# A GNN, MoE and routed-MLP megakernel on one core: the first expert's rows loaded early and finished by one-hot products; the last stage's row forms in halves, its relus' numbers loaded ahead, and one projection moved

## What is computed

```python
# step 2: experts; every token goes to one of E = 8, in the order of the tokens, at most C = 640 of each
idx = jnp.argmax(softmax(x @ gate_w + gate_b), axis=-1)
one_hot = jax.nn.one_hot(idx, E)
pos = (jnp.cumsum(one_hot, axis=0) * one_hot).sum(-1).astype(jnp.int32) - 1
buf = zeros((E, C, D)).at[idx, where(pos < C, pos, C)].set(x, mode='drop')
hmid = relu(einsum('ecd,edf->ecf', buf, w1) + b1)
ybuf = einsum('ecf,efd->ecd', hmid, w2) + b2          # then gathered back, times the probability
# step 3: x = x + adj @ (layernorm(x) * W)
# step 4: 64 segments of 64 rows, each with one of 16 experts in both layers
h = relu(flat @ Wi.T + bi)
for l in range(2):
    h = relu((h @ Ws[l] + bs[l]) + (h @ Wr[l, route].T + br[l, route]) + h)
out = h @ Wo.T + bo
```

## Time and profile before

| | |
|---|---|
| three runs | 974.94, 978.54, 980.27 us; median 978.54 |
| profiled execution | 976.39 us, its span 974.7 us |
| PE, DVE, ACT, POOL busy | 97%, 59%, 36%, 20% of the span |
| granted PE clock, mean | 0.988 of full speed |

### The profile page before, as it was taken

The page is one execution under the profiler, slowest core; times in us unless marked ns, Lnnn a source line. Parts: engine busy times, 40 slices in busy tenths (PEclk is TensorE's granted clock), DMA queues, the critical chain, the costliest instruction groups (busy, mean ns, idle before and its releaser), DMA issues.

```text
span 974.7 us, 15621 instructions
## 1 busy us (share of the span) xinstructions
PE 949.3 (97%) x4730; PEld 546.1 (56%) x4738; DVE 572.9 (59%) x1603; ACT 351.0 (36%) x845; POOL 195.3 (20%) x216
## 2 busy tenths in 40 slices
PE   8999999999999999999999899989999999999997
PEld 4555555555555544444443488834666666666665
DVE  5434234234224366777667388557886776877834
ACT  3554564564561022221111254414123333333242
POOL 3210010010010121122222246543120111102101
PEclk9999999999999999999999799979999999999999
DMA  9995784484303698988878257637998989989761
GB/s 354 422 412 198 320 345 174 172 346 195 151 1 136 261 374 318 348 313 318 317 293 357 75 167 244 209 90 287 380 375 323 371 319 341 353 317 360 231 185 52
DMA packets 64625, 263.26 MB, mean 270 GB/s; under 512 B 8852, under 2 KB 24920, under 8 KB 52246
## 3 DMA queue, kind: packets, MB, share of 16 engines
q1 hardware_dynamic: 61398, 257.69, 70.2%
q0 software_dynamic: 2864, 4.39, 1.3%
q10 hardware_dynamic: 272, 0.13, 0.0%
HBM read 244.37 MB, written 20.01 MB: 271 GB/s over the span
## 4 chain that ended last, share of the span: by engine, by line
PE 74%; DVE 9%; issue 5%; DMA 4%; DVEq 3%; ACT 3%; POOL 1%; ACTq 0%; another core or an unknown queue 0%; SPq 0%; POOLq 0%
PE PA L1893 22%; PE PA L2126 17%; PE PA L1873 11%; PE O L2064 3%; PE O L2230 3%; PE O L1942 3%; DMA disp_d<-work 2%; ACT U L800 2%; PE O L1914 2%; PE SM L2230 1%; PE SR L2230 1%; PE T L2241 1%; PE PA L1860 1%; PE O L1904 1%; PE O L2207 1%
## 5 line engine op out<-in xcount | busy, mean ns | idle before, releaser
L1893 PE MATMUL PA<-ring,S 128*128 128x512 f32 x512 | 229.0, 596 | 2.8 <-DMA ring<-in_adj_cols 2.3
L1873 PE MATMUL PA<-ring,U 128*128 128x512 f32 x512 | 223.3, 593 | 0.1
L1873 PEld LDWEIGHTS PA<-ring,U 128*128 128x128 f32 x512 | 96.0, 190 | 113.9 <-issue 113.8
L1893 PEld LDWEIGHTS PA<-ring,S 128*128 128x128 f32 x512 | 96.6, 191 | 105.3 <-issue 101.5
L2127 PE MATMUL PA<-ring 128*64 128x256 f32 x560 | 129.4, 380 | 0.0
L710 ACT ACTIVATE work<-ring 128x2048 int8<-128x2048 f32 x64 | 122.3, 1910 | 8.9 <-issue 4.7
L2126 PE MATMUL PA<-ring,S 128*64 128x256 f32 x448 | 105.4, 381 | 0.6 <-DVE ring L1704 0.6
L2126 PE MATMUL PA<-ring 128*64 128x256 f32 x336 | 80.6, 379 | 0.0
L2126 PEld LDWEIGHTS PA<-ring,S 128*64 128x64 f32 x448 | 60.0, 137 | 33.3 <-issue 3.9
L2127 PEld LDWEIGHTS PA<-ring 128*64 128x64 f32 x560 | 75.9, 137 | 0.0
L766 ACT ACTIVATE work<-work 128x128 f32<-128x128 f32 x112 | 33.2, 297 | 107.1 <-DVE work L1369 107.1
(11 more groups left out here) (305 smaller groups left out, 1448.1 us busy)
## 6 DMA issues: line engine op xcount, KB each, us to landing
ring<-in_adj_cols SPq DMA_DIRECT2D x52, 2048.0 KB, 9.7
ring<-in_adjT_cols SPq DMA_DIRECT2D x32, 2048.0 KB, 8.9
ring<-w_d SPq DMA_DIRECT2D x128, 256.0 KB, 3.7
ring<-in_adj_cols SPq DMA_DIRECT2D x8, 1024.0 KB, 14.2
ring<-in_Wr SPq DMA_DIRECT2D x4, 2048.0 KB, 8.9
w_d<-ring SPq DMA_DIRECT2D x8, 1024.0 KB
work<-in_w SPq DMA_DIRECT2D x16, 256.0 KB
disp_d<-U SPq DMA_DIRECT2D x4, 650.0 KB, 19.1
```

The source lines that it names most:

```text
L1873: mm = nc.tensor.matmul(out_T[:, :], X[:, t * D:(t + 1) * D], ring[slot][t // HT][:, (t % HT) * BW:(t % HT + 1) * BW], start=n == 0, stop= ...
L1893: mm = nc.tensor.matmul(PA[k % 2][:, :], S[:, t * D:(t + 1) * D], ring[slot][t // HT][:, (t % HT) * BW:(t % HT + 1) * BW], start=t == 0, s ...
```

## The change

1. **First expert.** When the scatters of the first seven blocks have landed, SP loads expert 0's slots (the rows of seven blocks; the last block's are still zero) into what was `gate_rows`. PE turns these five tiles with ordinary products into T[0], T[1] right after `tail_c`, ahead of the one `keep_warm` and `tail_d` (`early_turn`). POOL writes 0..639 into `e_slots` (iota) once the second layer's products are done, and the last block's four scatters now also wait for the early load. After `idx`, DVE compares the slots of each of the last block's four tiles with 0..639 (four comparisons, 128x640, `e_late`). PE, after `tail_d` and two `keep_warm` products, adds the last block's rows into T[0], T[1] by products with these one-hot rows (`late_rows`: for each tile 512 and 128 columns). The twelve `keep_warm` products and `turn_rows(0, 0)` go. SP waits for `late_rows` before it loads expert 1's weights. Expert 1's rows are turned in the middle of expert 0's second layer, not ahead of it. DVE adds two slices of shared weights ahead of the first expert, then one after each of experts 0 to 5.
2. **Row forms** are made in two halves: the first 16 tiles after `moments_y`, the second 16 after block 1's first quarter forms.
3. **Relus' numbers**: `relu_group` reads all four numbers ahead of its wait.
4. **Last block**: the `keep_warm` between the halves goes; `out_proj(7)` moves from ahead of layer 1 to behind `turn_routed(8, 1)`, into O[0]; block 8's layers both use SR and SM; `out_rows3(7)` moves behind layer 1's relus on DVE; the addition of the variance's epsilon moves from POOL to DVE.

```diff
             sp (after the loads of Wr)
+            sp.wait_ge(s_sc, 16 * BT * (NB - 1))
+            sp.dma_start(tiles(early_rows, CT, ROW), disp_t[:, 0:CT, :]).then_inc(s_early, 16)
             sp.wait_ge(s_sc, 16 * NT)
...
             load_rows(1, 1)
+            sp.wait_ge(s_xTp, 1)
             load_weights(1, 1)
             pool (step2)
+                    if nth == 2 * NB - 1:
+                        pool.wait_ge(s_agg2, NB)
+                        nc.gpsimd.iota(e_slots, pattern=[[1, CAP]], base=0, ...).then_inc(s_slots, 1)
                 if k == NB:
                     pool.wait_ge(s_rows, 1)
+                    pool.wait_ge(s_early, 16)
             dve (route)
+                if k == NB:
+                    nc.vector.scalar_tensor_tensor(slot_all, over, NOWHERE, slot_f, ALU.mult, ALU.add)
+                    dve.wait_ge(s_slots, 1)
+                    for t in range(BT):
+                        nc.vector.tensor_scalar(e_late[t], e_slots, slot_all[:, t:t + 1], None, ALU.is_equal).then_inc(s_late, 1)
...
-            for i in range(4):
+            for i in range(2):
                 add_self(i)
...
-                if e + 4 < NS:
-                    add_self(e + 4)
+                if e + 2 < NS:
+                    add_self(e + 2)
             pe (last2)
                 tail_c(k)
+                early_turn()
                 keep_warm(1, S[:, 0:BW], PA[0])
                 tail_d(k)
+                keep_warm(2, S[:, 0:BW], PA[0])
+                late_rows()
+            def early_turn():
+                pe.wait_ge(s_early, 16)
+                for q in range(CT):
+                    nc.tensor.matmul(slots_of(q), early_rows[:, q * ROW:q * ROW + D], ident[:, :], start=q % BT == 0, stop=False, ...)
+            def late_rows():
+                pe.wait_ge(s_rows, 1)
+                for t in range(BT):
+                    pe.wait_ge(s_late, t + 1)
+                    row = rows[:, t * ROW:t * ROW + D]
+                    nc.tensor.matmul(T[0][:, :], row, e_late[t][:, 0:BW], ...)
+                    last = nc.tensor.matmul(T[1][:, 0:CAP - BW], row, e_late[t][:, BW:CAP], ...)
+                last.then_inc(s_xTp, 1)
-            keep_warm(12, S[:, 0:BW], PA[0])
-            turn_rows(0, 0)
             pe (last3)
                 turn_hn3_half(0)
-                keep_warm(1, S[:, 0:BW], PA[1])
                 turn_hn3_half(1)
                 h0_half(0)
                 h0_half(1)
-                out_proj(NB - 1)
                 layer(k, 0)
                 turn_routed(k, 0)
                 turn_routed(k, 1)
+                out_proj(NB - 1)
                 layer(k, 1)
             dve (last stage)
-            row_forms()
+            row_forms(0)
             sum_forms(1, 0)
             cross_forms(1, 0)
             second_forms(1, 0)
             third_forms(1, 0)
+            row_forms(1)
             act (relu_group)
+                slots = [n % SB for n in range(g * SH, (g + 1) * SH)]
+                chosen = [act.value_load(...) for s in slots]
+                act.wait_ge(s_rt, (k - 1) * NG + g + 1)
+                for s, e in zip(slots, chosen):
```

More of the change, by code:

```diff
@@ L171, in build @@
         assert at + BW <= WORK
+        early_rows = gate_rows[:, 0:CT * ROW]
+        slot_all = limit
         BY_ROWS = range(1, NB)
@@ L189, in build @@
         e_hm = U[:, CAP:(1 + FK) * CAP]
+        e_late = [U[:, CAP * (1 + t):CAP * (2 + t)] for t in range(BT)]
+        e_slots = U[:, CAP * 5:CAP * 6]
         e_y = [R[:, CAP * i:CAP * (i + 1)] for i in range(2)]
@@ L622, in _ @@
             load_rows(1, 1)
+            sp.wait_ge(s_xTp, 1)
+            alone(sp)
             load_weights(1, 1)
@@ L844, in relu_group @@
                 dst = (h_b, h_a)[l]
[L845 to L850, removed]
+                slots = [n % SB for n in range(g * SH, (g + 1) * SH)]
+                chosen = [act.value_load(route_sb[0:1, ds((k - 1) * SB + s, 1)], min_val=0, max_val=E2 - 1) for s in slots]
+                act.wait_ge(s_rt, (k - 1) * NG + g + 1)
+                alone(act)
+                for s, e in zip(slots, chosen):
                     for m in range(KH):
@@ L1040, in _ @@
                 some = slice(h * H2, (h + 1) * H2)
-                inv_sqrt(H2, mv8[:, some, 1], s_mv4, NB + h, s_rstd4, first_power + NB + h, ve[:, some], rstd[:, some])
+                pool.wait_ge(s_mv4, NB + h)
+                alone(pool)
+                nc.gpsimd.tensor_tensor(rstd[:, some], ve[:, some], neg_half[:, 0:1].to_broadcast([P, H2]), ALU.pow).then_inc(s_rstd4, 1)
             store_rows(NB - 1)
@@ L1654, in last_hn3 @@
                     dve.drain()
-                    stats(lambda t: x3[:, t * D:(t + 1) * D], (h + 1) * H2, h * H2).then_inc(s_mv4, 1)
+                    stats(lambda t: x3[:, t * D:(t + 1) * D], (h + 1) * H2, h * H2)
+                    dve.drain()
+                    some = slice(h * H2, (h + 1) * H2)
+                    nc.vector.tensor_scalar(ve[:, some], mv8[:, some, 1], LN_EPS, None, ALU.add).then_inc(s_mv4, 1)
                 for h in range(2):
@@ L1670, in last_hn3, with row_forms @@
                         relu_rows(NB, g)
-            def row_forms():
-                dve.wait_ge(s_wkept, 16 * NS)
+                    if l == 0:
+                        out_rows3(NB - 1)
+            def row_forms(half):
+                some = slice(half * NQ // 2, (half + 1) * NQ // 2)
+                needed = [c for c, (lo, hi) in enumerate(CHUNKS) if lo < (half + 1) * HT][-1]
+                if half == 0:
+                    dve.wait_ge(s_wkept, 16 * NS)
+                    alone(dve)
+                dve.wait_ge(s_hid2, needed - FIRST + 1)
                 alone(dve)
-                dve.wait_ge(s_hid2, len(CHUNKS) - FIRST)
-                alone(dve)
-                nc.vector.tensor_tensor(T1, B12, B11, ALU.subtract)
-                nc.vector.tensor_tensor(T3, B22, B12, ALU.subtract)
+                nc.vector.tensor_tensor(T1[:, some, :], B12[:, some, :], B11[:, some, :], ALU.subtract)
+                nc.vector.tensor_tensor(T3[:, some, :], B22[:, some, :], B12[:, some, :], ALU.subtract)
                 dve.drain()
-                nc.vector.tensor_tensor(T2, B22, T1, ALU.subtract)
+                nc.vector.tensor_tensor(T2[:, some, :], B22[:, some, :], T1[:, some, :], ALU.subtract)
                 dve.drain()
-                nc.vector.tensor_tensor(T4n, B21, T2, ALU.subtract).then_inc(s_tform, 1)
+                nc.vector.tensor_tensor(T4n[:, some, :], B21[:, some, :], T2[:, some, :], ALU.subtract).then_inc(s_tform, 1)
             def sum_forms(b, qq):
@@ L2055, in expert @@
                                      start=True, stop=True).then_inc(s_h1, 1)
-                if more:
+                if more and e > 0:
                     turn_rows(1 - par, rnd + par)
@@ L2066, in expert @@
                     mm.then_inc(s_yp, 1)
+                    if e == 0 and lo == 0:
+                        turn_rows(1, 0)
             def last_expert(e, par):
```

30 lines of the change are left out of this document (24 added, 6 removed).

## The result

Twelve runs of each: the changed kernel takes 971.84 us in the median (968.96 to 974.77), the kernel before 976.46 (974.41 to 980.27); the medians lie 4.6 us apart. The ratio on record is 0.9943, 95% interval [0.9927, 0.9959], which is 5.6 us (4.0 to 7.1). Measured again later, beside the kernel before on chip 15, it was 970.14 against 972.87, 0.9971 [0.9958, 0.9983], 2.8 us. Between the two profiled executions the difference is 972.94 against 976.39.

What follows compares the result with a forecast made beforehand. PE was taken to bound the kernel, busy 97% of the span. First expert 5.2, row forms 0.6 and last block 0.8 sum to 6.6 us, subtracted from 977.5 for 970.9 us; range 966.5 to 978.

Steps and rivals of the forecast that it cites:

- First expert, 5.2: At expert 0, early load, early turn and late rows replace warm products and turn: gain 5.2 us, 4.0 with late rise.
- the rise I had put at 545.8: During the first expert's early work, PE's clock returns to full near 545.8, since unbroken work begins at 540.4.
- the 24 warm instructions: Ahead of expert 0: 13.19 us in all, first 5 at half clock; each 0.44 us at full, 0.87 at half.
- four slow comparisons: DVE's comparisons for the last block's tiles at 1.5 us each, not 0.6: done by 551.7, gain about 3.2 us.
- So the rest of the program should follow earlier by the whole amount.: After expert 0, everything from expert 1 on starts earlier by the first expert's full gain, 5.2 us.
- Row forms, 0.6: At PE's first split product, the wait for the second forms goes: gain 0.6 us, zero if adj's quarter lands late.
- Relus' numbers, "beside a full PE: nothing": In blocks 1 to 6, ACT's loads of the relus' numbers lie beside a full PE: no gain or loss.
- Last block, 0.8: Layer 1 starts 2.2 us sooner without the projection, 1.4 is given back: gain 0.8 us, bounds 0 and 1.5.
- The first, the clock in the last block: Without the last block's warm product the clock falls for ten microseconds: gain shrinks to 2.6, 974.9 us; chance 0.18.
- The second, gain lost at expert 1: Expert 1's rows or weights land 5 us later than read and PE waits there: 976.1 us; chance 0.10.
- The third, a low clock that reaches expert 0: Half clock holds through the late rows, and expert 0 loses another 2.7 us: 1.8 slower, 979.3 us; chance 0.10.

Runs made afterwards that it cites:

- e10: Kernel before with first expert's part, row forms in halves and relus' loads ahead only in the last two groups, last block as before: 967.73 us, 0.9949.
- e11: Kernel before with only the last block's part (projection moved, epsilon on DVE), warm product kept between the turns: 973.53 us, 1.0008.
- e3: Kernel before with the first expert's part alone: 970.27 us, 0.9965.
- e9: Changed kernel, warm product back, relus' loads ahead only in last two groups, last expert's second layer for part two before first layer for part three: 968.91 us, 0.9965.

## Why the prediction was right, and where not

The forecast was 970.9 us, 6.6 us under 977.5. The measured median, 971.84, lies 0.9 us from it, but under a kernel before that took 976.46: the gain is 4.6 us by the medians, 5.6 by the ratio and 2.8 on chip 15. The stages give 3.7. The sign and the main term are right; that the total comes so close is in part luck, since one loss of 2.1 us was put at nothing and others, of 0.55 and 1.8 us, and a gain of 1.2 us were not foreseen.

- **First expert, 5.2.** Right step by step: early load awaited until 540.33 (540.4), `tail_d` 1.46 late (1.65), comparisons 0.47 apart and 0.55 long (0.6), the first one there at 546.84 (546.9), `late_rows` 4.56 us to 551.54 (4.5 to 551.6), first layer 5.22 sooner. The clock rose at about 544.7 (0.91 over 544 to 548), 1.1 us before the rise I had put at 545.8; it gained nothing more, since `late_rows` waits for DVE. Two slips in the working changed nothing: of the 24 warm instructions six ran at half clock, not five (five and nineteen add up to 12.7 us, not to 13.19), and four slow comparisons would have ended at 552.3, not 551.7.
- **"So the rest of the program should follow earlier by the whole amount."** This step failed three times, in both directions. Expert 1's rows were turned ahead of expert 0's second layer, while PE would have waited for ACT; now PE waits 0.62 us there and does the turn inside that layer, so expert 1 starts only 4.67 us sooner (562.71 in place of 567.38). The last expert's later first products had waited 1.19 us for ACT, and that wait went too (I had not looked that far): 6.17 us at the end of PE's experts. Then DVE's wait for the last expert's second part grew from 3.17 to 4.84 (its distance from PE's record from 2.57 to 4.34, 1.8 us lost): products of block 0 started 4.37 us sooner. On chips 15 and 0 that distance grows alike, from 0.23 to 1.06 without the part to 2.73 to 2.79 with it; why is open. In stage A, profiles with the part show 109.2 to 111.7 us, those without 112.4 to 115.8; the part's gain there is some 2.5 us (e10 beside e11, both on chip 0) to 6 us (e3 beside the kernel before).
- **Row forms, 0.6.** Right: 0.69; stage B is 31.34 to 31.38 in the four profiles without them and 30.68 to 30.69 in eight of the ten with them (the quarter forms were never late).
- **Relus' numbers, "beside a full PE: nothing".** Wrong, and the largest miss: 2.1 us lost. I costed the loads on PE's side and did not read ACT's order: ACT's timeline before shows the copy, then relus with loads between them. The change adds no instruction to ACT; it moves three loads of each group from between the relus to ahead of them, still behind the copy, and from the copy to the second group's end ACT then takes 0.51 us more. I had named no work that hides it but PE's, and PE itself was next in line for the relus.
- **Last block, 0.8.** Right in mechanism, 0.54 in size. Layer 1 came 1.88 us sooner behind the warm products (2.2), 1.34 was given back (1.4). In its place stood what the prediction named: DVE's normalised half is the late one (949.97 and 951.01 both wait for DVE), and ε on DVE takes 0.14 (0.1). DVE doesn't wait for block 7's store at the end. That the relus' loads alone would take the same gain I had not seen.
- **Rivals.** The first, the clock in the last block, is half true: it falls in three profiles of five, at 1.5 to 1.7 us and not at 4, since the clock is back by the end of layer 1's first products. The second, gain lost at expert 1: PE has no wait there; the 0.55 us above are lost ahead of it. The third, a low clock that reaches expert 0: full from 548 on.

Why the medians scatter around 3.7: the kernel before took 976.5 us in the first measurement and on chip 7, and 972.2 to 973.4 on chips 0 and 15, with the same code. The anchor differs by up to 4.6 us between profiles, in steps that go with the clock of the first 100 us. The long delays of the late signal (2.57 without the first expert's part, 4.33 and 4.34 with it) are from the first measurement and chip 7, the short ones (0.23 to 1.06, 2.73 to 2.79) from chips 15 and 0. How much each adds to the medians was not separated.

## What to carry to other kernels

A load moved ahead of a wait gains only what the engine idles between the load's new place and that wait; ahead of the load, read the engine's own order: what stands before it decides when it starts, and work that had been hidden between two operations may now stand in front of both. When a change is worth a few tenths of a per cent, cut the profiles at instructions that all kernels share and compare the distances: here that gave 1.9 to 2.5 us for the relus' loads from any pair of one profile with them and one without, where medians of one kernel moved by 4. Read the granted clock in each stage beside its length, since a half-clock spell can lie on either side of a cut. A warm product that looks useless between two turns may be what holds the clock; take it out only where the profile shows a full clock without it more than once.

## What the runs showed of the hardware

- Reading four numbers into ACT's registers, back to back and with nothing to hide them, took 1.07 to 2.04 us of ACT's time (the "issue" idle ahead of the relus in five profiles); one between two relus left a gap of 0.23 to 0.54.
- With PE doing two turns (0.44 us each) in some 2.6 us, the granted clock fell to half in three of five profiles and stayed full in two; where one warm product of 1.02 us lay between the turns, it was full in all nine.
- Signals of PE's products behind the last expert came up to 5.2 us after the recorded end of the products (changed kernel: 628.74 to 633.98), and in e9 1.4 us apart where the records are 0.22 apart; the cause is open. In such a place the waits of DVE and ACT, not PE's records, tell when a product is done.
- Four comparisons of 128x640 with one number per row took DVE 1.94 us, one every 0.47 us and 0.55 us each.
